# The first stage of a two-layer kernel: logits, sigmoid and choice of the next block are issued ahead of the old block's down product

## The reference

```python
xn = _layernorm(x)
qkv = xn @ w_attn                                   # (256, 768)
logits = xt @ gate_w.T                              # xt = xn, 4096 tokens; 8 experts
_, idx = jax.lax.top_k(logits + beta, 2)
probs = jax.nn.sigmoid(jnp.take_along_axis(logits, idx, axis=-1))
sh = silu(xt @ shared_gate_w) * (xt @ shared_up_w)  # 256 -> 512
shared_out = sh @ shared_down_w                     # 512 -> 256
```

## Time and profile before

| | us |
|---|---|
| three runs | 3474.88, 3474.18, 3465.55 |
| their median | 3474.18 |
| the profiled execution: its own time | 3470.55 |
| its span, first to last instruction | 3468.8 |
| mean granted TensorE clock | 0.970 |

### The profile page before, as it was taken

One profiled execution on the slowest core, in us unless ns is written; L12 is line 12 of the kernel. 1 busy time (PEld: TensorE's weight loads), 2 busy tenths in 40 slices (PEclk: granted clock), 3 DMA queues, 4 the chain that ended last, 5 costly groups with the idle time before them and its releaser, 6 DMA issues. The chain is left out here.

```text
span 3468.8 us, 61116 instructions
## 1 busy us (share of the span) xinstructions
PE 3204.0 (92%) x19814; PEld 1290.4 (37%) x19815; DVE 2811.6 (81%) x4921; ACT 2315.2 (67%) x3660; POOL 1650.6 (48%) x2104
## 2 busy tenths in 40 slices
PE   7787799999999999999999999878999999999987
PEld 4554466652222222222222222252334333333333
DVE  5666533569999999999999999366989999899997
ACT  3344333337888888788888878757867777777763
POOL 2233500003443433444443434305888888888885
PEclk9899999999999999999999999988999999999998
DMA  4332311111121111011111110041222222222221
GB/s 152 111 115 93 96 57 57 51 44 35 36 60 41 38 36 33 28 31 34 35 35 35 35 32 26 12 158 56 71 74 67 78 79 68 77 83 68 75 77 50
DMA packets 160889, 211.63 MB, mean 61 GB/s; under 512 B 32324, under 2 KB 108364, under 8 KB 160604
## 3 DMA queue, kind: packets, MB, share of 16 engines
q1 hardware_dynamic: 141340, 172.51, 16.0%
q0 software_dynamic: 8512, 18.76, 1.7%
q10 hardware_dynamic: 10752, 16.78, 1.4%
HBM read 154.48 MB, written 52.69 MB: 60 GB/s over the span
## 5 line engine op out<-in xcount | busy, mean ns | idle before, releaser
L1415 ACT ACTIVATE prob<-psS 128x1024 f32<-128x1024 f32 (+3 forms) x1280 | 1104.1, 906 | 281.0 <-PE psS L1599 271.5
L1465 DVE TENSOR_REDUCE pmax<-psR 128x1 f32<-128x512 f32 x1674 | 1056.5, 683 | 81.2 <-PE psR L1541 47.8
L2241 POOL TENSOR_TENSOR hc<-h_d,crep 128x512 f32<-128x512 f32 x512 | 647.0, 1272 | 187.5 <-DVE h_d L2470 138.0
L1541 PE MATMUL psR<-kslab,qslab 48*128 48x512 bf16 (+3 forms) x2480 | 652.8, 352 | 22.3 <-DVE pmax L1465 14.1
L1614 PE MATMUL psVo<-prob,vaug 128*32 128x512 f32 (+3 forms) x5120 | 630.8, 546 | 1.6 <-ACT ov L1419 0.8
L1599 PE MATMUL psS<-qslab,kslab 51*128 51x512 bf16 (+3 forms) x2560 | 533.2, 353 | 40.6 <-ACT prob L1415 22.7
L2470 DVE TENSOR_TENSOR_SCAN h_d<-a,state,psU 128x512 f32<-128x512 f32 x384 | 489.4, 1275 | 0.0
L1330 POOL TENSOR_SCALAR_AFFINE_SELECT prob<-prob 128x256 f32<-128x256 f32 (+1 forms) x512 | 213.3, 420 | 534.8 <-ACT prob L1415 534.8
L2460 DVE TENSOR_TENSOR psU<-dtx,psX 128x512 f32<-128x512 f32 x512 | 356.0, 695 | 90.0 <-PE psX L2620 38.9
L1541 PEld LDWEIGHTS psR<-kslab,qslab 48*128 48x128 bf16 x2480 | 187.3, 94 | 629.7 <-DVE pmax L1465 465.3
L2373 ACT ACTIVATE a<-dt,a_neg 128x512 f32<-128x512 f32 x512 | 366.9, 724 | 54.3 <-DVE h_d L2470 53.4
(11 more groups left out here) (351 smaller groups left out, 5145.9 us busy)
## 6 DMA issues: line engine op xcount, KB each, us to landing
crep<-c_rows_d SPq DMA_DIRECT2D x256, 256.0 KB, 3.1
x_e<-rows_d SPq DMA_DIRECT2D x72, 128.0 KB, 2.0
y_d<-y SPq DMA_DIRECT2D x72, 128.0 KB, 1.7
q_d<-parts SPq DMA_DIRECT2D x48, 128.0 KB, 2.3
k_d<-parts SPq DMA_DIRECT2D x48, 128.0 KB, 2.3
qslab<-q_d SPq DMA_DIRECT2D x60, 96.0 KB
kslab<-k_d SPq DMA_DIRECT2D x60, 96.0 KB
wg<-n_L_ffn_gate_proj_w_dram ACTq DMA_DIRECT2D x8, 512.0 KB, 3.9
```

Of the source, the lines that this page charges most:

```text
L1415: act.activation(prob[g % BUFS][:, :, off:BLK], psS[g % 2][:, :, off:BLK], ACT.Exp).then_inc(prob_ready, 1)
L1465: dve.tensor_reduce(into[:, lo:lo + (count - 1) * NEXT + 1:NEXT], psR[at % BANKS][:, 0:count * w].rearrange("p (n w) -> p n w", w=w), AX.X ...
L1541: ins = pe.matmul(dst[:, m * w:(m + 1) * w], qslab[u][rows, i * P:(i + 1) * P], kslab[u][rows, ch * BLK:ch * BLK + w], start=(m == 0), sto ...
L2241: pool.tensor_tensor(hc[:, g % CR], h[:, g % HR], crep[:, g // PAIR % SPR], ALU.mult).then_inc(hc_ready, 1)
```

## The change

On all three engines the steps that decide about block n + 1 are issued at the end of block n, ahead of `down(n)` on PE. `turn(n + 1)` moves ahead of the product u3, and `logits(n + 1)` stands behind u3. On ACT `copy_turned(n + 1)` goes ahead of the last weight cast and `scores(n + 1)` follows that cast, ahead of `copy_shared(n)`. On DVE `choose(n + 1)` and `weight_max(n + 1)`, in this order, stand behind `hidden(n, 3)`. `values(n)` stays behind `down(n)`. The first block's steps stand ahead of the loops.

```diff
@@ vector
             dve.wait_ge(gate_in, 32 + CREDIT)
+            weight_max(0)
+            choose(0)
             for n in range(NBLK):
-                weight_max(n)
-                choose(n)
                 cut(n, 0)
                 weight_row(n)
...
                 hidden(n, 3)
+                if n + 1 < NBLK:
+                    choose(n + 1)
+                    weight_max(n + 1)
@@ scalar
             load_expert(1)
+            scores(0)
             for n in range(NBLK):
-                scores(n)
                 copy_rows(n, 0)
...
                 gate(n, 3)
+                if n + 1 < NBLK:
+                    copy_turned(n + 1)
                 high_weights(n, 2)
                 if n + 1 < NBLK:
-                    copy_turned(n + 1)
+                    scores(n + 1)
                 copy_shared(n)
@@ tensor
             turn(0)
+            logits(0)
             for n in range(NBLK):
-                logits(n)
                 product(n, "q", 0)
...
                 product(n, "g", 3)
+                if n + 1 < NBLK:
+                    turn(n + 1)
                 product(n, "u", 3)
                 if n + 1 < NBLK:
-                    turn(n + 1)
+                    logits(n + 1)
                 down(n)
                 values(n)
```

## The result

The changed kernel takes 3438.4 us (median of five runs, 3436.32 to 3447.71) against 3473.14 for the kernel before: ratio 0.9914, 95% interval 0.9895 to 0.9934. The ratio goes with the means of the five runs on each side, 3441.32 and 3471.05, which lie 29.7 us apart; the medians lie 34.7 apart. The forecast was 3442, range 3424 to 3460. The profiled execution took 3436.32 us, with a span of 3434.5 against 3468.8 and a mean granted clock of 0.972 against 0.970.

What follows compares the result with a forecast made beforehand. A first-stage block was bound by a loop through TensorE, DVE and GpSimd. Logits 11.9, the spread_max hole 12.9 and clock 4.8 sum to 29.6 us; 3470.55 becomes 3441.0, forecast 3442, own range 3430 to 3452, wider range 3424 to 3460.

Steps and rivals of the forecast that it cites:

- The period: Time of one first-stage block on TensorE, predicted to be 41 to 43 us instead of 45 to 48.
- The hole ahead of `spread_max`: TensorE's wait for diag_r in each block: an earlier choose cuts 13.5 us over seven blocks to 0.6, gaining 12.9 us.
- Logits: On TensorE, logits move from behind values into the wait ahead of down: 1.70 us seven times, 11.9 us gained.
- The clock: Up products behind the spread_max hole ran partly at 1.2 GHz; without the hole 4.8 us return, bounds 0 and 4.8.
- Down's cost: TensorE's down product was taken as unchanged, with bounds of 17.5 us gained and 6 us lost.
- the rival that the clock stays up in down: Less idle keeps TensorE's clock up in the down product: 17.5 us more gained, 3424 us; chance 0.10.
- the slower one: TensorE stays at 1.2 GHz through all of down and values: 55 us lost, 3496 us; chance 0.04.
- The margins: Ahead of down, normalize ends 0.77 us before turn asks, and ScalarE's cast 0.7 us before GpSimd's third subtraction starts.
- beyond it each microsecond costs one per block: Past the 0.7 us between the end of ScalarE's last weight cast and GpSimd's third subtraction, delay costs its length every block.
- The large hole: TensorE's wait ahead of down, released by hidden, was to shrink from 6.92 us to 4.9 us (237.9 to 242.8).
- POOL's end plus 2.99 us: Start of down: GpSimd's subtractions end, then the rest of the cut and hidden(n, 3) take 2.99 us.
- Without the cover they would cost the 1.70 again, so the change would be neutral there: Without TensorE's 6.92 us idle ahead of down, logits placed there would cost their 1.70 us again and gain nothing.

Runs made afterwards that it cites:

- e1: Changed kernel with the next block's sigmoid moved back behind copy_values and the weight loads, and DVE's maxima again ahead of choose; ratio to the kernel before 1.0018.
- e4: Kernel before, with GpSimd's three subtractions held back until hidden(n, 3) is done; ratio to the kernel before 0.9811.
- e5: Changed kernel with GpSimd's subtractions held back only until the fourth cut is done; 3386.64 us, ratio to the kernel before 0.976.
- e8: Changed kernel with turn(n + 1) behind u3 again, logits still ahead of down; ratio to the kernel before 0.9916.
- e3: Changed kernel with GpSimd's three subtractions held back until hidden(n, 3) is done; ratio to the kernel before 0.9787.
- e2: Kernel before, with only TensorE's spread_max moved behind the up product u0 and rank; ratio to the kernel before 0.9932.
- e10: Kernel before with the edits of e2 and e5, logits, sigmoid and choose left where they were; 3384.81 us, ratio to the kernel before 0.9754.
- e7: Changed kernel with spread_max behind the up product u0 and rank, the edit of e2; ratio to the kernel before 0.9893.
- e9: e5 with turn(n + 1) behind u3 again, the edit of e8; ratio to the kernel before 0.982.
- e6: e5 with logits(n + 1) behind down instead of ahead of it, and the sigmoid behind copy_shared; ratio to the kernel before 0.9786.

## Why the prediction was right, point by point

*The period.* Predicted 41 to 43 us; measured 42.1 and 43.2 by turns (the longer ones, just outside, are those in which down took 10.2 us), and 44.6 for the first. The sum of 29.6 us stands against 30.1 at the landmark and 29.7 between the means of the runs. Term by term the rows give 11.9 for logits (seven times 1.70), 12.9 for the hole and 4.6 for the clock, 29.4 together. The median stands 34.7 us lower, which is 5 us more than the mean does; nothing in the first stage accounts for these.

*The hole ahead of `spread_max`.* Predicted 0.6 us left over; 0.6. The cut starts 2.55 us into the block, by ScalarE's copy, where 2.63 was predicted. The gain reached POOL, whose subtractions start 2.0 us sooner in the block (predicted 1.9), and so it was not eaten by the large hole.

*Logits.* Query products follow values directly, and logits are hidden in the hole: 1.70 us a block. Here the form of the sum was too simple. It has 11.9 us for logits and 12.9 us for the hole as separate terms. e1 showed that the first is nothing without the early sigmoid: the sigmoid's chain behind values was as long as before and set the cut. Terms on two branches that join are a maximum, not a sum; they added up here because the change shortened both branches.

*The clock.* The 4.8 us behind the hole came back as 4.6 (65.6 to 61.0). Down's cost was taken as unchanged, between bounds of 17.5 us gained and 6 lost, and the sum was, 75.6 to 75.7. So the rival that the clock stays up in down did not happen, nor did the slower one. That it came out to 0.1 us is luck: the prediction gave no reason for this point between the bounds, and block by block down did move, from 8.58 to 10.08 us before to about 9.1 and 10.2 by turns. The Trainium skill's rule, "TensorE: Matmul & The Clock Gate", Part 1, that the clock follows how busy TensorE has lately been, pointed the right way only when the hole went altogether (7.17 us in e4, 7.15 in e5).

*The margins.* Normalize ends 0.76 us ahead of turn (214.26, 215.02), predicted 0.77; the cast ends 0.8 ahead of the third subtraction, predicted 0.7. The step "beyond it each microsecond costs one per block" did not hold in e8: the margin was crossed by 0.25 us and no cost showed, since a pause of POOL lets one held instruction through. No run crosses it by more.

*The large hole.* Predicted 4.9 us, measured 4.64 to 4.85 in the seven blocks with logits, its cause confirmed by e3 to e5. The prediction took down's start as POOL's end plus 2.99 us as if that were fixed. It held in the changed kernel (221.70 + 2.98 = 224.68), but e2 (1.34 us) shows that it depends on how much of the cut is still undone when POOL starts.

*The lock.* The Trainium skill, "SBUF — State Buffer", Who interferes with whom, has an exclusive lock for one instruction. The rows agree on the lock and on its victims (copies, and operations with two SBUF inputs; `hidden`, with one input in PSUM, is not held in e5). They differ on its length: three subtractions back to back held a copy for 6.94 us, and only a pause of 0.25 us let one DVE instruction in. The held cast's row even starts 0.35 us ahead of the first subtraction's (215.06, 215.41), so the start of a row does not tell which of the two will be held.

*Without cover.* "Without the cover they would cost the 1.70 again, so the change would be neutral there" speaks of the logits alone. e10 and e5, where the hole ahead of `spread_max` and the large hole are gone from both, differ by 2.7 us at the landmark, so near neutral. e4 and e3 differ by 3.1, although e4 has the hole ahead of `spread_max` and e3 has not; the 10 us of clock in down and the 3 us of gaps, which the prediction did not have, took most of that back.

What stays open: which property of the gap with logits behind it brings the clock down, beyond that both are needed in these runs, and whether the 4.7 us by which e7 is ahead of the changed kernel at the landmark (2.4 of it are in down) are more than the difference between two executions.

## What to carry to other kernels

Before moving work off a loop, name the engine whose instruction is *held*, not only the one that idles: here a wait of 2 us on GpSimd (e5) gave 52 us on top of the 35 of the whole reordering, and moving one line on TensorE (e2) gave 20 of the reordering's 30 us at the landmark. Two edits that remove the same hole don't add up (e2, e7), and an edit that needs a second one is worth nothing without it (e1: logits without the early sigmoid). Narrow matmuls moved into a wait are free only as long as the wait is there; once it is gone, a short gap with them behind it cost 1.7 us of clock or more, mostly in the next product (e3, e9).

## What was not expected of the hardware

- A gap of 0.47 to 1.16 us followed by 1.8 us of 8-column matmuls brought the clock to 1.2 GHz in all 13 cases, inside the next product in ten and already in these matmuls in three (e3, e9: the product took 8.57 to 10.16 us instead of 7.15); a gap of 0.95 us alone (e6) or such matmuls without a gap (e5) brought it down in none.
- GpSimd instructions back to back kept DVE's copy waiting over all three of them, 6.94 us, and one DVE instruction passed in a pause of 0.25 us (e8). Holding GpSimd back by 2 us took the wait away (e5).
- The rest of the kernel, identical in all twelve profiles, took from 3063.9 to 3074.9 us.
